# Storing layer 1's sums of x and no-op rows once, and a half-size block first among layer 0's experts

## The chip, the core and the metric

The kernel runs on one core of a Trainium2 chip. The metric is device time of one execution, in microseconds (us). Engines are named as in the profile: PE (TensorE matmuls) and PEld (its weight loads), DVE (VectorE), ACT (ScalarE), POOL (GpSimd) and SP (SyncE, which here only issues DMAs; its queue is SPq). SBUF is the on-chip memory, PSUM the accumulators that PE writes.

## What is computed

Two gated transformer layers over x (8 x 256 tokens of 256 numbers, 2048 tokens). The part that matters here, cut from the reference:

```python
x = x + tanh(g_xattn[0]) * L0_xattn(layernorm(x), ctx, ...)
x = x + tanh(g_ffn[0]) * L0_ffn(layernorm(x), ...)      # 8 experts, top 2, no capacity
x = x + tanh(g_xattn[1]) * L1_xattn(layernorm(x), ctx, ...)
x = x + tanh(g_ffn[1]) * L1_ffn(layernorm(x), ...)      # 7 experts and a no-op one, top 2

# L1_ffn: expert i takes its first cap = 256 tokens
h = relu(einsum('ceh,ehi->cei', inputs, experts_inter))
out = einsum('cei,eih->ceh', h, experts_out) * in_w[..., None]
combined = zeros_like(x_flat).at[used_idx].add(out.reshape(-1, hidden))
combined = combined + x_flat * (noop_w * noop_mask)[:, None]
```

So the result of layer 1 is x, plus the scaled no-op rows (normalised x times the weight of the eighth expert), plus the experts' rows, added token by token.

## The kernel before

Each layer is an attention phase and then a route and experts phase. A token tile is 128 tokens, on the 128 partitions; there are 16 (`TT`). `shared["x"]` (x_sb in the profile) holds x and `shared["xr"]` its normalised rows, 16 x 256 numbers on each partition.

**Attention** ends, for each of 8 batches, with `store_router_rows`: SP stores the normalised rows (L269, to the table normalised_weighted) and then x itself (L271), in layer 0 to x1, in layer 1 to out. The phase's last waits on SP are for those stores (L291, L292).

**Routing** (`route_phase`) is a chain of small DVE steps that finds for every slot of every block the token that belongs there (`token_of`). In layer 1 ACT also scales xr by the weight of the no-op expert (L1258), 16 instructions. The scratch tiles of this phase lie in x_sb, which in the kernel before is free by then because x is in memory, and in a small tile "more".

**Experts** (`expert_phase`) runs over blocks. A block has one expert's weights (w1 and w2, 1 MB each) and 256 rows (two gathers of 128) or, in layer 0 alone, 128 rows (one gather): a small block. Layer 0 has 16 full blocks and 7 small ones, and `SMALL_AT` says at which places of the 23 the small ones stand. Layer 1 has 7 full blocks. In a block b

- POOL gathers the rows of xw into `xe` (`load_x`, L1556), two buffers, and after the block scatters the weighted outputs with an adding DMA (`add_to_tokens`, L1581);
- PE turns the rows (`turn`, L1786), does the first product into ps_h (L89 to L91, each product split in three) and the second into ps_y. Its order is: first product of b, within it the turn of b + 1, then the second product of b - 1;
- ACT and DVE split weights, inputs and hidden rows in a high and a low part: ACT makes the high parts (L1616, L1624, L1656) and the activation (L1632, L1635), DVE the rest (L1688, L1699, L1711, L1713, L1757);
- the weights come by gathers of POOL in layer 0 (L1161) and by DMAs of SP in layer 1 (L1538 for w1, L1541 for w2), each as soon as the buffer two blocks back has been split.

No scheduler sets an order: each engine's program is written out, as above, and engines meet in semaphores. In layer 1 POOL's program begins with `load_x(0)`, `load_x(1)`, `load_x(2)`, then four DMAs of 512 KB that add the scaled no-op rows to out in memory (L1596), then for each b `load_x(b + 3)` and `add_to_tokens(b)`. The first `add_to_tokens` waits until the four DMAs have landed (`out_added`).

The functions that the change touches, and what calls them, follow with the line numbers of the profile.

Of the kernel before, what the change touches and what calls it, by code (L numbers as in the profile page):

```python
# [13 lines left out]
P = 128  # L14
B, S, D = 8, 256, 256
N = B * S
# [12 lines left out]


FULLS = 16
SMALL_AT = (3, 7, 10, 13, 16, 19, 22)
L0_BLOCKS = FULLS + len(SMALL_AT)
CT = 4
HALVES = 2 * FULLS + len(SMALL_AT)
# [65 lines left out]
def attention_phase(nc, layer, shared, dram):  # L101
# [4 lines left out]
    with ExitStack() as ctx:  # L106
# [105 lines left out]
        def _(sp):  # L212
# [48 lines left out]
                    sp.dma_start(dram["xw"][unused_rows, D:D + E], shared["zeros"][:, 0:E]).then_inc(xr_stored, 16)  # L261
            xr_dst = dram["xw"][0:N, 0:D].rearrange("(t p) d -> p t d", p=P)

            x_dst = dram["out" if layer else "x1"][0:N, :].rearrange("(t p) d -> p t d", p=P)

            def store_router_rows(b):
                tiles = slice(b * QT, b * QT + QT)
                wait_routed(sp, b)
                sp.dma_start(xr_dst[:, tiles, :], xr[:, tiles, :]).then_inc(xr_stored, 16)  # L269
                sp.wait_ge(x_done, b + 1)  # L270
                sp.dma_start(x_dst[:, tiles, :], x[:, tiles, :]).then_inc(x_stored, 16)  # L271

            load_context(4)
            maxima_to_slots(0)
# [14 lines left out]
            store_router_rows(B - 2)  # L289
            store_router_rows(B - 1)  # L290
            sp.wait_ge(xr_stored, 16 * (B + (0 if layer else 2 * QT)))  # L291
            sp.wait_ge(x_stored, 16 * B)  # L292

        @block.gpsimd
        def _(pool):
# [841 lines left out]
def expert_buffers(nc, ctx, layer):  # L1137

    sem = semaphores(nc, ctx)

    def sb(name, shape, dt=F32):
        return ctx.enter_context(nc.sbuf_tensor(f"{name}_w{layer}", shape, dt))

    def pair(name, shape):
        return [sb(f"{name}{i}", shape) for i in range(2)]

    buffers = {"w1_raw": pair("w1_raw", [P, KC * F + (0 if layer else FC)]),
               "w2_raw": pair("w2_raw", [P, FC * D + (0 if layer else D)]),
               "w1_ld": [sem(f"w1_ld{i}_w{layer}") for i in range(2)], "w2_ld": [sem(f"w2_ld{i}_w{layer}") for i in range(2)]}
    buffers["comb"] = sb("comb", [P, TT, E])  # L1150
    if layer:
        buffers["out_added"], buffers["noop_scaled"] = sem("out_added_w1"), sem("noop_scaled_w1")
    else:
        buffers["block_is"] = sb("block_is", [P, L0_BLOCKS, E])
    return buffers
# [10 lines left out]
def route_phase(nc, ctx, layer, shared, dram, buffers, tiles):  # L1166
# [2 lines left out]
    tg = shared["tanh_g"][:, 2 + layer:3 + layer]  # L1169


    spare = [shared["x"][:, :, :].rearrange("p a b -> p (a b)"), tiles["more"][:, :]]
    room = [TT * D, MORE]
    taken = [0, 0]

    def sb(name, shape, dt=F32, home=0):
        n = math.prod(shape[1:])
        words = n if dt in (F32, I32) else n // 2
        at = taken[home]
        taken[home] += words  # L1180
        assert taken[home] <= room[home], name
        ap = spare[home][:, at:at + words]
        if dt != F32:
            ap = ap.bitcast(dt)
        if len(shape) == 3:
            ap = ap.rearrange("p (a b) -> p a b", b=shape[2])
        if len(shape) == 4:
            ap = ap.rearrange("p (a b c) -> p a b c", b=shape[2], c=shape[3])
        return ap
# [21 lines left out]
    low, smaller = sb("low", [P, TT, E]), sb("smaller", [P, L0_BLOCKS])  # L1211
    before, first = sb("before", [P, 2, E, E]), sb("first", [P, E])
    base, place, valid = sb("base", [P, E]), sb("place", [P, TT, E]), sb("valid", [P, TT, E])
    past, blk_row, blk_expert = sb("past", [P, L0_BLOCKS, 2 * E], home=1), sb("blk_row", [P, L0_BLOCKS]), sb("blk_expert", [P, L0_BLOCKS])
    weight, slot = ([sb(f"{n}{i}", [P, TT], dt) for i in range(2)] for n, dt in (("weight", F32), ("slot", I32)))
    quotient, remainder = sb("quotient", [P, 2, TT], I32), sb("remainder", [P, 2, TT], I32)
    half_of, lane_of = sb("half_of", [P, 2, TT], F16), sb("lane_of", [P, 2, TT], F16)

    is_half = [sb(f"is_half{i}", [P, HALVES, TT], F16, i) for i in range(2)]
    token_at = [sb(f"token_at{i}", [P, HALVES, TT], F16) for i in range(2)]  # L1220
    is_lane = [sb(f"is_lane{i}", [P, P, TT], F16, i) for i in range(2)]
    unused = sb("unused", [P, HALVES])


# [248 lines left out]
def expert_phase(nc, ctx, layer, shared, dram, buffers):  # L1473
# [15 lines left out]
    def sem(name):  # L1489
        return new_sem(f"{name}_e{layer}")  # L1490
# [12 lines left out]
    if layer == 0:  # L1503
# [10 lines left out]
    w1_hi, w1_ready, w2_hi, w2_ready, xe_ps, xe_hi, xe_ready, h_ps, hid_ready, h_hi, h_ready, y_ps, y_ready = (  # L1514
        sem(n) for n in ("w1_hi", "w1_ready", "w2_hi", "w2_ready", "xe_ps", "xe_hi", "xe_ready", "h_ps",
                         "hid_ready", "h_hi", "h_ready", "y_ps", "y_ready"))
    last_ps, last_ready = sem("last_ps"), sem("last_ready")
    NP = FC // 2

    def loaded(b):  # L1520
# [3 lines left out]
        return 16 * sum(order[c][2] for c in range(b % 2, b + 1, 2))  # L1524

    listed, comb_stored = sem("listed"), sem("comb_stored")
    tiles = {"more": sb("more", [P, MORE]), "ps_h": ps_h, "ps_y": ps_y, "listed": listed, "comb_stored": comb_stored}

    def sync_part(sp):
        if layer:  # L1530

            for b in range(2):
                sp.wait_ge(xe_ld[b], passed(b))

            def load_weights(b):
                if b + 2 < blocks:
                    sp.wait_ge(w1_ready, b + 1)
                    sp.dma_start(w1_raw[b % 2][:, :], dram["w1"][(b + 2) * P:(b + 3) * P, :]).then_inc(w1_ld[b % 2], 16)  # L1538
                if b + 1 < blocks:
                    wait(sp, w2_ready, b)  # L1540
                    sp.dma_start(w2_raw[(b + 1) % 2][:, :],  # L1541
                                 dram["w2"][(b + 1) * P:(b + 2) * P, :]).then_inc(w2_ld[(b + 1) % 2], 16)

            for b in range(blocks):
                load_weights(b)
        for b in (blocks - 2, blocks - 1):
            sp.wait_ge(y_out[b % 2], passed(b))

    def pool_part(pool):
# [20 lines left out]
        def add_to_tokens(b):  # L1570
            if b < blocks - 1:
                pool.wait_ge(y_ready, b + 1)
            if b:
                pool.wait_ge(y_out[(b - 1) % 2], passed(b - 1))
            elif layer:
                pool.wait_ge(buffers["out_added"], 16 * (TT // CT))
            for q in range(order[b][2]):
                t = order[b][1] + q
                if b == blocks - 1:
                    pool.wait_ge(last_ready, q + 1)  # L1580
                pool.indirect_dma_start(  # L1581
                    out=dram["out" if layer else "x1"], out_offset=bass.IndirectOffsetOnAxis(ap=shared["token_of"][:, t:t + 1], axis=0),
                    in_=y[b % 2][:, q, :], in_offset=None, compute_op=ALU.add).then_inc(y_out[b % 2], 16)
# [3 lines left out]
        load_x(0)  # L1587
        load_x(1)
        if layer:
            load_x(2)  # L1590

            out_dst = dram["out"][0:N, :].rearrange("(t p) d -> p t d", p=P)
            for c in range(TT // CT):
                tiles = slice(c * CT, c * CT + CT)
                pool.wait_ge(buffers["noop_scaled"], c * CT + CT)
                pool.dma_start(out_dst[:, tiles, :], shared["xr"][:, tiles, :],  # L1596
                               accum_op=ALU.add).then_inc(buffers["out_added"], 16)
            for b in range(blocks):
# [353 lines left out]
```

## Time and profile before

| | us |
|---|---|
| median of 3 runs | 845.72 |
| lowest and highest | 845.16 and 845.79 |
| the profiled execution | 845.71 |
| its span in the trace | 844.0 |
| PE busy in it | 752.9 (89%) |
| DVE busy | 603.9 (72%) |
| ACT busy | 478.4 (57%) |
| POOL busy | 382.4 (45%) |

The span is 1.7 us less than that execution's own time; this rest lies outside the trace. The trace shows layer 0's attention up to 210 us, its routing up to 233, its experts up to 492, layer 1's attention up to 710, its routing up to 730 and its experts to the end. Times in the trace are from the span's start. The busy shares are averages over these stages. What a change is worth is read from the stage, from which wait ends last there.

### The profile page before, as it was taken

The numbers are of one execution on the slowest core, as the hardware profiler recorded it, in microseconds if no ns is written. First come the engines' busy times: TensorE is split into PE (matmuls) and PEld (weight loads), VectorE is DVE, ScalarE is ACT, GpSimd is POOL, SyncE is SP. The second block draws the span as 40 slices with busy tenths as digits, with TensorE's granted clock in tenths as the row PEclk, the third lists the DMA queues.
The fourth block names the chain that finished last, engine by engine and source line by source line (L and its number), as shares of the span: only waits on it lengthen the run. The fifth ranks groups of instructions, "written<-read, shape, count | busy, mean of one in ns | idle before, by whom it ended". The sixth has DMA issues, their size and how long they took to land. (4 is left out here: it accounts for less than half of the span.)

```text
span 844.0 us, 17413 instructions
## 1 busy us (share of the span) xinstructions
PE 752.9 (89%) x6872; PEld 636.0 (75%) x6872; DVE 603.9 (72%) x1212; ACT 478.4 (57%) x722; POOL 382.4 (45%) x379
## 2 busy tenths in 40 slices
PE   6999999999469999999999948999999998295995
PEld 5666667667369999999999946666677667295995
DVE  4777777753769998998998916777777734774882
ACT  3376666753056777777676603676667661553640
POOL 6465444112145766666666326645551130252532
PEclk9999999999779999999999979999999999587998
DMA  7001000010377888888888336001000013398642
GB/s 231 15 21 40 27 27 23 9 50 32 98 276 218 243 259 251 256 251 253 254 254 253 74 58 192 14 15 40 27 28 27 28 43 117 97 304 220 165 86 28
DMA packets 47697, 103.45 MB, mean 123 GB/s; under 512 B 9952, under 2 KB 38240, under 8 KB 39936
## 3 DMA queue, kind: packets, MB, share of 16 engines
q0 software_dynamic: 18912, 67.56, 28.0%
q1 hardware_dynamic: 28704, 34.78, 12.3%
q8 instruction: 55, 0.90, 0.4%
q14 instruction: 26, 0.21, 0.1%
HBM read 84.22 MB, written 17.83 MB: 121 GB/s over the span
## 5 line engine op out<-in xcount | busy, mean ns | idle before, releaser
L598 DVE TENSOR_REDUCE mx_a<-ps_max_a 128x2 f32<-128x512 f32 x256 | 164.2, 685 | 35.5 <-PE ps_max_a L844 35.2
L89 PE MATMUL ps_h_e<-xe_t_e,w_e 128*128 128x256 f32 (+1 forms) x480 | 137.9, 287 | 6.0 <-DVE xe_t_e L1757 6.0
L450 ACT ACTIVATE prob_a<-ps_st_a 128x2048 f32<-128x2048 f32 x64 | 120.1, 1876 | 29.1 <-PE ps_st_a L863 28.7
L90 PE MATMUL ps_h_e<-xe_t_e,w_e 128*128 128x256 f32 (+1 forms) x480 | 134.9, 281 | 0.0
L91 PE MATMUL ps_h_e<-xe_t_e,w_e 128*128 128x256 f32 (+1 forms) x480 | 134.9, 281 | 0.0
L89 PE MATMUL ps_y_e<-w_e,h_e 128*128 128x256 f32 x424 | 118.5, 279 | 0.0
L90 PE MATMUL ps_y_e<-w_e,h_e 128*128 128x256 f32 x424 | 118.0, 278 | 0.0
L91 PE MATMUL ps_y_e<-w_e,h_e 128*128 128x256 f32 x424 | 117.9, 278 | 0.0
L89 PEld LDWEIGHTS ps_h_e<-xe_t_e,w_e 128*128 128x128 f32 x480 | 93.0, 194 | 8.2 <-DVE xe_t_e L1757 8.2
L91 PEld LDWEIGHTS ps_h_e<-xe_t_e,w_e 128*128 128x128 f32 x480 | 92.7, 193 | 0.0
L90 PEld LDWEIGHTS ps_h_e<-xe_t_e,w_e 128*128 128x128 f32 x480 | 92.7, 193 | 0.0
L844 PE MATMUL ps_max_a<-k_r_a,q_r_a 32*128 32x512 f32 x256 | 82.8, 513 | 4.0 <-DVE mx_a L598 1.1
L318 POOL TENSOR_SCALAR r_var_eps_a<-r_mean_var_a 128x2 f32<-128x2 f32 x16 | 3.6, 228 | 180.0 <-DVE r_mean_var_a L625 180.0
L1161 POOL DMA_INDIRECT w_raw_w<-L_w,block_row x46 | 48.5, 1055 | 80.6 <-DVE b_e L1704 55.4
L1581 POOL DMA_INDIRECT x<-y_e,token_of x39 | 68.6, 1760 | 30.7 <-ACT y_e L1647 17.4
L1556 POOL DMA_INDIRECT xe_e<-normalised_weighted,token_of x53 | 61.7, 1163 | 45.4 <-DVE token_of L1467 28.0
L89 PEld LDWEIGHTS ps_y_e<-w_e,h_e 128*128 128x128 f32 x424 | 79.9, 188 | 0.0
L91 PEld LDWEIGHTS ps_y_e<-w_e,h_e 128*128 128x128 f32 x424 | 79.9, 188 | 0.0
L90 PEld LDWEIGHTS ps_y_e<-w_e,h_e 128*128 128x128 f32 x424 | 79.8, 188 | 0.0
L1713 DVE TENSOR_TENSOR h_e<-hid_e,h_e 128x512 fp32r<-128x512 f32 (+1 forms) x120 | 76.1, 634 | 4.1
L863 PE MATMUL ps_st_a<-q_s_a,k_s_a 32*128 32x256 f32 x1024 | 78.0, 395 | 0.3
L1635 ACT ACTIVATE hid_e<-ps_h_e,b_e 128x256 f32<-128x256 f32 (+1 forms) x184 | 71.0, 445 | 8.1 <-PE ps_h_e L91 7.6
(236 smaller groups left out, 1756.0 us busy)
## 6 DMA issues: line engine op xcount, KB each, us to landing
w_raw_w<-L_w SPq DMA_DIRECT2D x14, 1024.0 KB
ctx_raw_a<-ctx_t SPq DMA_DIRECT2D x16, 256.0 KB, 4.2
normalised_weighted<-xr SPq DMA_DIRECT2D x16, 256.0 KB, 2.2
x_sb<-x SPq DMA_DIRECT2D x8, 256.0 KB
x_sb<-x SPq DMA_DIRECT2D x2, 1024.0 KB, 8.6
x<-x_sb SPq DMA_DIRECT2D x8, 256.0 KB, 2.5
out<-x_sb SPq DMA_DIRECT2D x8, 256.0 KB, 2.5
out<-xr POOLq DMA_DIRECT2D x4, 512.0 KB, 21.9
```

Of the source, the lines that this page charges most:

```text
L89: pe.matmul(out, lhs[0], rhs[0], start=start, stop=False)
L90: pe.matmul(out, lhs[1], rhs[0], start=False, stop=False)
L91: return pe.matmul(out, lhs[0], rhs[1], start=False, stop=stop)
L450: act.activation(prob[n % 2][:, :, :, :], ps_st[:, :, :, :], ACT.Exp, scale=HD ** -0.5).then_inc(prob_ready, 1)
L598: dve.tensor_reduce(mx[:, q, h:h + HG + 1:HG], ps_max[j][:, :, :], AX.X, ALU.max).then_inc(max_done, 1)
L844: pe.matmul(ps_max[j][:, :, :], q_r[b % 2][r:r + 32, c, q * P:(q + 1) * P], k_r[b % 2][r:r + 32, c, :, :], start=True, stop=True).then_inc ...
L863: ins = pe.matmul(ps_st[:, g, kt, :], k_s[b % 3][c % 2][rows, c // 2, kt * P:(kt + 1) * P], q_s[b % 3][c % 2][rows, c // 2, :], start=True ...
L1161: pool.indirect_dma_start(out=buffers[which + "_raw"][b % 2][:, :], out_offset=None, in_=dram[which], in_offset=bass.IndirectOffsetOnAxis( ...
L1556: pool.indirect_dma_start(out=xe[b % 2][:, q, :], out_offset=None, in_=dram["xw"], in_offset=bass.IndirectOffsetOnAxis(ap=shared["token_of ...
L1581: pool.indirect_dma_start(out=dram["out" if layer else "x1"], out_offset=bass.IndirectOffsetOnAxis(ap=shared["token_of"][:, t:t + 1], axis=0),
L1635: ins = act.activation(hid[jp % 2][:, j, 0:w], ps_h[jp % RB][:, j, 0:w], ACT.Gelu, bias=b1[b % 2][:, 2 * jp + j:2 * jp + j + 1])
L1713: dve.tensor_tensor(h[b % 2][1][:, js, 0:w], hid[jp % 2][:, :, 0:w], h[b % 2][0][:, js, 0:w].bitcast(F32), ALU.subtract).then_inc(h_ready, 1)
```

## The change

It has four parts.

1. `SMALL_AT` goes from (3, 7, 10, 13, 16, 19, 22) to (0, 4, 8, 12, 15, 18, 22).
2. Layer 1's attention no longer stores x to out.
3. In layer 1's experts, the no-op rows are added to x in SBUF by POOL, four additions of 128x1024 (`add_rows`), and the sums are stored to out by SP, four plain DMAs of 512 KB. The first `add_to_tokens` waits for these (`out_stored`).
4. So that x_sb stays intact, the scratch tiles of routing lie elsewhere (in "more", in hid, y and xe of the experts, and in w2_raw's second buffer), in both layers.

```diff
-SMALL_AT = (3, 7, 10, 13, 16, 19, 22)
+SMALL_AT = (0, 4, 8, 12, 15, 18, 22)
...
                 sp.dma_start(xr_dst[:, tiles, :], xr[:, tiles, :]).then_inc(xr_stored, 16)
-                sp.wait_ge(x_done, b + 1)
-                sp.dma_start(x_dst[:, tiles, :], x[:, tiles, :]).then_inc(x_stored, 16)
+                if layer == 0:
+                    sp.wait_ge(x_done, b + 1)
+                    sp.dma_start(x_dst[:, tiles, :], x[:, tiles, :]).then_inc(x_stored, 16)
...
-            sp.wait_ge(x_stored, 16 * B)
+            if layer == 0:
+                sp.wait_ge(x_stored, 16 * B)
...
-    spare = [shared["x"][:, :, :].rearrange("p a b -> p (a b)"), tiles["more"][:, :]]
-    room = [TT * D, MORE]
-    taken = [0, 0]
+    spare = [tiles["more"][:, :]] + [tile[:, :, :].rearrange("p a b -> p (a b)") for tile in tiles["later"]]
+    spare.append(buffers["w2_raw"][1][:, 0:FC * D])
+    room = [MORE] + [math.prod(tile.shape[1:]) for tile in tiles["later"]] + [FC * D]
+    taken = [0] * len(spare)
...
+            out_dst = dram["out"][0:N, :].rearrange("(t p) d -> p t d", p=P)
             for b in range(blocks):
                 load_weights(b)
+                if b == 0:
+                    for c in range(TT // CT):
+                        sp.wait_ge(out_summed, c + 1)
+                        tiles = slice(c * CT, c * CT + CT)
+                        sp.dma_start(out_dst[:, tiles, :], shared["x"][:, tiles, :]).then_inc(buffers["out_stored"], 16)
...
             elif layer:
-                pool.wait_ge(buffers["out_added"], 16 * (TT // CT))
+                pool.wait_ge(buffers["out_stored"], 16 * (TT // CT))
...
         if layer:
-            load_x(2)
-
-            out_dst = dram["out"][0:N, :].rearrange("(t p) d -> p t d", p=P)
-            for c in range(TT // CT):
+
+            def add_rows(c):
                 tiles = slice(c * CT, c * CT + CT)
                 pool.wait_ge(buffers["noop_scaled"], c * CT + CT)
-                pool.dma_start(out_dst[:, tiles, :], shared["xr"][:, tiles, :],
-                               accum_op=ALU.add).then_inc(buffers["out_added"], 16)
+                pool.tensor_tensor(shared["x"][:, tiles, :], shared["x"][:, tiles, :], shared["xr"][:, tiles, :],
+                                   ALU.add).then_inc(out_summed, 1)
+
+            add_rows(0)
+            add_rows(1)
+            load_x(2)
+            add_rows(2)
+            add_rows(3)
             for b in range(blocks):
                 load_x(b + 3)
                 add_to_tokens(b)
```

How this moves instructions, at three places. In the names, xe0_e1 is the first buffer of gathered rows in layer 1's experts, y0_e1 a block's weighted output.

POOL at the start of layer 1's experts, before:

```order
L1845 UNCONDITIONAL_BRANCH
L1556 DMA xe0_e1<-normalised_weighted,token_of 128x264 x2
L1556 DMA xe1_e1<-normalised_weighted,token_of 128x264 x2
L1556 DMA xe0_e1<-normalised_weighted,token_of 128x264 x2
L1596 DMA out<-xr 128x4x256 x4
L1556 DMA xe1_e1<-normalised_weighted,token_of 128x264 x2
L1581 DMA out<-y0_e1,token_of 2304x256 x2
```

And in the changed kernel:

```order
L1858 UNCONDITIONAL_BRANCH
L1565 DMA xe0_e1<-normalised_weighted,token_of 128x264 x2
L1565 DMA xe1_e1<-normalised_weighted,token_of 128x264 x2
L1603 TENSOR_TENSOR x_sb<-x_sb,xr 128x1024 x2
L1565 DMA xe0_e1<-normalised_weighted,token_of 128x264 x2
L1603 TENSOR_TENSOR x_sb<-x_sb,xr 128x1024 x2
L1565 DMA xe1_e1<-normalised_weighted,token_of 128x264 x2
L1590 DMA out<-y0_e1,token_of 2304x256 x2
```

Four adding DMAs between the third and the fourth pair of gathers are gone; two POOL additions stand ahead of the third pair and two ahead of the fourth.

SP from the start of layer 1's routing on, before (w_raw is a block's raw weights):

```order
L1240 DMA normalised_weighted<-comb_w1 128x16x8
L1538 DMA w1_raw0_w1<-L1_w1 128x2048
L1541 DMA w2_raw1_w1<-L1_w2 128x2048
L1538 DMA w1_raw1_w1<-L1_w1 128x2048
L1541 DMA w2_raw0_w1<-L1_w2 128x2048
```

And in the changed kernel:

```order
L1243 DMA normalised_weighted<-comb_w1 128x16x8
L1541 DMA w1_raw0_w1<-L1_w1 128x2048
L1544 DMA w2_raw1_w1<-L1_w2 128x2048
L1554 DMA out<-x_sb 128x4x256 x4
L1541 DMA w1_raw1_w1<-L1_w1 128x2048
L1544 DMA w2_raw0_w1<-L1_w2 128x2048
```

The four stores, each with a wait for one of POOL's additions, stand ahead of the weights w1 of block 3 and all later ones.

POOL at the start of layer 0's experts, before:

```order
L1161 DMA w1_raw1_w0<-L0_w1,block_row 128x2056
L1556 DMA xe0_e0<-normalised_weighted,token_of 128x264 x2
L1556 DMA xe1_e0<-normalised_weighted,token_of 128x264 x2
L1161 DMA w1_raw0_w0<-L0_w1,block_row 128x2056
L1161 DMA w2_raw1_w0<-L0_w2,block_row 128x2304
```

And in the changed kernel:

```order
L1163 DMA w1_raw1_w0<-L0_w1,block_row 128x2056
L1565 DMA xe0_e0<-normalised_weighted,token_of 128x264
L1565 DMA xe1_e0<-normalised_weighted,token_of 128x264 x2
L1163 DMA w1_raw0_w0<-L0_w1,block_row 128x2056
L1163 DMA w2_raw1_w0<-L0_w2,block_row 128x2304
```

Block 0 has one gather instead of two, and everything behind it on POOL is issued one gather earlier.

## Rows read from the trace of the kernel before

**Rows 1.** The page's first line.

```profile
span 844.0 us, 17413 instructions
```

**Rows 2.** Waits from 725 us on: who waited for whom, us in total, times, longest.

```profile
POOL out L1581 <- DMA out<-xr: 22.7, 1, 22.7
PE ps_x_e L1786 <- DMA xe_e<-normalised_weighted,token_of: 16.8, 2, 10.2
```

**Rows 3.** The chain that ended last: start us, us, what.

```profile
748.25 24.28 DMA xe_e<-normalised_weighted,token_of
```

**Rows 4.** Timeline of POOL, layer 1: start us, us, instruction, [idle before <-releaser].

```profile
735.45 0.94 POOL L1556 DMA_INDIRECT xe_e<-normalised_weighted,token_of  x1 [0.30 <-issue]
738.58 0.94 POOL L1556 DMA_INDIRECT xe_e<-normalised_weighted,token_of  x1 [2.18 <-DVE xe_t_e L1757]
...
740.77 5.37 POOL L1596 DMA_DIRECT2D out<-xr  x4
746.44 1.50 POOL L1556 DMA_INDIRECT xe_e<-normalised_weighted,token_of  x1 [0.30 <-issue]
748.25 1.81 POOL L1556 DMA_INDIRECT xe_e<-normalised_weighted,token_of  x1 [0.30 <-issue]
```

**Rows 5.** Tile xe_e, the two gathers that POOL issued from 738 to 741.

```profile
DMA to landing us min/median/max: 6.4/6.6/6.8
```

**Rows 6.** DMA issues of the page: count, KB each, median us to landing.

```profile
out<-xr POOLq DMA_DIRECT2D x4, 512.0 KB, 21.9
```

**Rows 7.** Stretches: length, busy us (count) by engine, PE clock, DMA share, GB/s.

```profile
core 0: us, PE busy (x) PEld busy (x) DVE busy (x) ACT busy (x) POOL busy (x), PEclk, DMA share, GB/s
750.66:786.32 35.66, 25.45 (x202) 25.25 (x201) 23.16 (x36) 13.99 (x20) 7.74 (x6) 0.86 0.81 222
786.32:797.87 11.55, 11.55 (x102) 11.55 (x101) 10.40 (x17) 6.45 (x10) 6.76 (x5) 1.00 0.79 224
762.36:772.57 10.21, 0.00 (x1) 0.00 (x0) 4.66 (x7) 0.79 (x2) 0.00 (x0) 0.72 0.91 284
309.49:341.58 32.09, 31.77 (x276) 31.57 (x275) 29.61 (x55) 22.96 (x45) 21.21 (x16) 1.00 0.83 247
```

**Rows 8.** Timeline of PE, in both layers' experts.

```profile
238.67 1.13 PE L1786 MATMUL ps_x_e<-ident,xe_e 128*128 128x128 f32 x4 [5.68 <-DMA xe_e<-normalised_weighted,token_of]
261.40 0.38 PE L89 MATMUL ps_h_e<-xe_t_e,w_e 128*128 128x256 f32 x1 [0.85 <-DVE xe_t_e L1757]
757.96 0.28 PE L89 MATMUL ps_h_e<-xe_t_e,w_e 128*128 128x256 f32 x1
772.57 1.13 PE L1786 MATMUL ps_x_e<-ident,xe_e 128*128 128x128 f32 x4 [10.21 <-DMA xe_e<-normalised_weighted,token_of]
```

**Rows 9.** Timeline of DVE, layer 1 first, then a small block of layer 0.

```profile
741.96 0.74 DVE L1711 CAST h_e<-hid_e 128x512 fp32r<-128x512 f32 x1 [3.65 <-ACT hid_e L1632]
742.73 0.69 DVE L1713 TENSOR_TENSOR h_e<-hid_e,h_e 128x512 fp32r<-128x512 f32 x1
744.68 0.43 DVE L1711 CAST h_e<-hid_e 128x512 fp32r<-128x512 f32 x1 [0.59 <-ACT hid_e L1632]
756.82 0.69 DVE L1757 TENSOR_TENSOR xe_t_e<-ps_x_e,xe_t_e 128x512 fp32r<-128x512 f32 x1
276.99 0.30 DVE L1711 CAST h_e<-hid_e 128x256 fp32r<-128x256 f32 x1 [0.34 <-ACT hid_e L1635]
277.32 0.42 DVE L1713 TENSOR_TENSOR h_e<-hid_e,h_e 128x256 fp32r<-128x256 f32 x1
```

**Rows 10.** Groups of POOL by form: busy us, mean ns, idle before.

```profile
L314 POOL TENSOR_TENSOR x_sb<-x_sb,tgbo_a 128x512 f32<-128x512 f32 x16 | 20.4, 1283 | 0.7
```

**Rows 11.** Timeline of SP's queue in layer 1's experts.

```profile
739.14 0.43 SPq L1538 DMA_DIRECT2D w_raw_w<-L_w  x1
749.20 0.33 SPq L1541 DMA_DIRECT2D w_raw_w<-L_w  x1
```

**Rows 12.** Waits of SP's queue, whole span.

```profile
SPq L292 <- DMA out<-x_sb: 2.0, 1, 2.0
```

**Rows 13.** Timeline of POOL at the start of layer 0's experts.

```profile
233.81 1.69 POOL L1556 DMA_INDIRECT xe_e<-normalised_weighted,token_of  x1 [4.53 <-DVE token_of L1467]
235.80 0.95 POOL L1556 DMA_INDIRECT xe_e<-normalised_weighted,token_of  x1 [0.30 <-issue]
```

More of the change, by code:

```diff
@@ L262, in _ @@
             xr_dst = dram["xw"][0:N, 0:D].rearrange("(t p) d -> p t d", p=P)
-            x_dst = dram["out" if layer else "x1"][0:N, :].rearrange("(t p) d -> p t d", p=P)
+            x_dst = dram["x1"][0:N, :].rearrange("(t p) d -> p t d", p=P)
             def store_router_rows(b):
@@ L1151, in expert_buffers @@
     if layer:
-        buffers["out_added"], buffers["noop_scaled"] = sem("out_added_w1"), sem("noop_scaled_w1")
+        buffers["out_stored"], buffers["noop_scaled"] = sem("out_stored_w1"), sem("noop_scaled_w1")
     else:
@@ L1169, in route_phase, with sb @@
     tg = shared["tanh_g"][:, 2 + layer:3 + layer]
-    spare = [shared["x"][:, :, :].rearrange("p a b -> p (a b)"), tiles["more"][:, :]]
-    room = [TT * D, MORE]
-    taken = [0, 0]
-    def sb(name, shape, dt=F32, home=0):
+    spare = [tiles["more"][:, :]] + [tile[:, :, :].rearrange("p a b -> p (a b)") for tile in tiles["later"]]
+    spare.append(buffers["w2_raw"][1][:, 0:FC * D])
+    room = [MORE] + [math.prod(tile.shape[1:]) for tile in tiles["later"]] + [FC * D]
+    taken = [0] * len(spare)
+    def sb(name, shape, dt=F32):
         n = math.prod(shape[1:])
         words = n if dt in (F32, I32) else n // 2
+        home = [i for i in range(len(spare)) if taken[i] + words <= room[i]][0]
         at = taken[home]
         taken[home] += words
-        assert taken[home] <= room[home], name
         ap = spare[home][:, at:at + words]
@@ L1213, in route_phase @@
     base, place, valid = sb("base", [P, E]), sb("place", [P, TT, E]), sb("valid", [P, TT, E])
-    past, blk_row, blk_expert = sb("past", [P, L0_BLOCKS, 2 * E], home=1), sb("blk_row", [P, L0_BLOCKS]), sb("blk_expert", [P, L0_BLOCKS])
+    past, blk_row, blk_expert = sb("past", [P, L0_BLOCKS, 2 * E]), sb("blk_row", [P, L0_BLOCKS]), sb("blk_expert", [P, L0_BLOCKS])
     weight, slot = ([sb(f"{n}{i}", [P, TT], dt) for i in range(2)] for n, dt in (("weight", F32), ("slot", I32)))
@@ L1217, in route_phase @@
     half_of, lane_of = sb("half_of", [P, 2, TT], F16), sb("lane_of", [P, 2, TT], F16)
-    is_half = [sb(f"is_half{i}", [P, HALVES, TT], F16, i) for i in range(2)]
+    is_half = [sb(f"is_half{i}", [P, HALVES, TT], F16) for i in range(2)]
     token_at = [sb(f"token_at{i}", [P, HALVES, TT], F16) for i in range(2)]
-    is_lane = [sb(f"is_lane{i}", [P, P, TT], F16, i) for i in range(2)]
+    is_lane = [sb(f"is_lane{i}", [P, P, TT], F16) for i in range(2)]
     unused = sb("unused", [P, HALVES])
@@ L1516, in expert_phase @@
                          "hid_ready", "h_hi", "h_ready", "y_ps", "y_ready"))
-    last_ps, last_ready = sem("last_ps"), sem("last_ready")
+    last_ps, last_ready, out_summed = sem("last_ps"), sem("last_ready"), sem("out_summed")
     NP = FC // 2
@@ L1526, in expert_phase @@
     listed, comb_stored = sem("listed"), sem("comb_stored")
-    tiles = {"more": sb("more", [P, MORE]), "ps_h": ps_h, "ps_y": ps_y, "listed": listed, "comb_stored": comb_stored}
+    tiles = {"more": sb("more", [P, MORE]), "later": hid + y + xe, "ps_h": ps_h, "ps_y": ps_y, "listed": listed, "comb_stored": comb_stored}
     def sync_part(sp):
```

## The prediction, made before the changed kernel ran

> **What bounds the kernel now.** I read four views, from the end backwards. The chain that ended last has one link that is neither PE nor a short step: a gather of rows for the experts of layer 1, issued at 748.25, that is 24.28 us on its way [rows 3]. The waits of that stage say who paid: PE waited 10.2 us for such a gather, in one piece, and POOL 22.7 us for the adding DMAs of the no-op rows before it could scatter the first block [rows 2]. POOL's timeline shows the cause in its order: the gathers of block 3 (746.44 and 748.25) are issued right behind the four adding DMAs (740.77) [rows 4]. Those take a median of 21.9 us to land [rows 6], while the gathers issued two us ahead of them landed in 6.4 to 6.8 us, though a weight load of 1 MB, the last of three in a row, had been issued at 739.14 [rows 5, 11]. So the queue of adding DMAs is what the gathers sit behind, not the weights.
>
> What this costs is read from the stretches. From the turn of block 2 (750.66) to the turn of block 4 (786.32) are 35.66 us; one later block takes 11.55 us, with PE busy all of it and DVE 10.40 [rows 7]. Two blocks should be 23.1, so **12.6 us** are lost: 10.2 of idle PE, and 2.4 in the matmuls behind it, where the granted clock was down from 2.4 to 1.2 GHz (the mean over the idle stretch is already 0.72) [rows 7, 8]. Elsewhere in the expert stages PE is busy nearly throughout, so nothing but a PE gap is worth anything there. The reader should also see how little spare DVE has early on: block 2's first product starts at 757.96, and the DVE instruction that it needs last runs from 756.82 for 0.69, that is, until 757.5 [rows 8, 9]. The margin is 0.45 us.
>
> **Layer 1, what goes.** The four adding DMAs go from POOL's queue, 5.4 us of issuing with them [rows 4]. Without them the third pair of gathers runs as below, and the stall of 12.6 us goes if its data are there when PE reaches 762.4.
>
> **Layer 1, what comes.** Four additions of 128x1024 on POOL. The nearest row is an addition of 128x512 at 1.28 us [rows 10]; twice that is 2.56 each, 10.2 in all. Placed in POOL's order: the second pair of gathers ends at 736.4 [rows 4], so two additions run to 741.6. The third pair (block 2) is issued at 741.9 and 743.2 rather than 738.58; with 6.6 us to landing it is there by 749.8, ahead of the turn at 750.66, with 0.9 to spare. The other two additions run from 744.1 to about 749.7 with their waits, and the pair for block 3 is issued from 750.0 to 753.6 (at the 1.50 and 1.81 of rows 4). With up to 6.8 us to landing it is there by 758.7, ahead of 762.4. SP's stores wait for the additions, and the load of w1 for block 3 waits behind them: from 739.14 to about 750 [rows 11]. The w2 load behind it was issued at 749.20 anyhow and moves by 1 us. ACT first needs w1 of block 3 when it has begun block 2, around 759; two stores (1 MB) and this load at the 284 GB/s of rows 7 take 7 us, until 757. That is cover enough, but it is no large one: 1 us later per us that the additions slip beyond 2. All four stores land by then too, before the first scatter can start (760), so the wait of 22.7 us is worth nothing more by itself.
>
> **What the additions do to DVE** is the term that the trace does not show: no DVE instruction that reads two SBUF tiles runs there beside a POOL computation. The first two additions fall where DVE waits for PE (its instruction of 741.96 had idled 3.65 us) [rows 9]. The other two fall at 744.1, just as DVE begins the unbroken run of casts and subtractions that ends in the margin of 0.45. Lower bound: nothing, then the gain is all 12.6. Upper bound: the two engines exclude each other and DVE stands still for what of both additions falls in its run: 746.7 minus 744.7 for the first, 2.5 for the second, 4.5 us. The nearest row is a DVE cast beside POOL's DMA issues: 0.74 instead of 0.43, while POOL's own gather issues beside DVE's run took 1.50 and 1.81 instead of 0.94 [rows 4, 9]. Each delays the other, which looks like exclusion for as long as POOL touches SBUF; an addition touches it all the time. I take the upper bound, 4.5, less the margin 0.45: **a new PE gap of 4.1 us** ahead of block 2's first product (part of it may show ahead of block 0's second product, which waits for the same run). Layer 1's experts then gain 12.6 - 4.1 = **8.5 us**.
>
> The Trainium skill, page "SBUF — State Buffer", section "Who interferes with whom", says that a DVE instruction with two SBUF inputs and a GpSimd one that reads SBUF share a port pair, and that the one that starts second "fully blocks". By the 0.3 us of the row alone the gap would be nearly nothing; by the page it would be the 4.1 above. No row here shows a case of the page's own kind.
>
> **Layer 0, small block first.** Block 0 now needs one gather. The second was issued 2.0 us after the first, whose issue took 0.74 longer [rows 13], so the first should land some 1.25 us before 238.67, when PE started. Two transposes instead of four and half-width copies on ACT and DVE take off another 0.8 (the four took 1.13) [rows 8]. Then DVE bounds: block 2's first product waited 0.85 us for it at 261.40 [rows 8]. DVE's cast and subtraction take 0.30 + 0.42 in a small block instead of 0.43 + 0.69 [rows 9], 0.4 less, four times: 1.6. So 261.40 becomes about 257.7, 3.7 earlier. Not all of it is gain, since a small block's saving is spent here instead of at place 3: two full blocks and a small one took 32.09 us [rows 7], so a small one 32.09 - 23.1 = 9.0, 2.6 less than a full one. Net 3.7 - 2.6 = 1.1, and I take **1.2**. Bounds: -1.0, if the start does not come earlier, and 2.5, if PE and not DVE bounds again. How the other small blocks are spread costs nothing that the trace shows: PE is busy 31.77 of the 32.09, and the last block is small in both.
>
> **The rest.** SP's last wait of the attention, for the store of x, was 2.0 us [rows 12]. The engines' own work ended about when it did, so I count 0.2 (bounds 0 and 2.0). The eight stores of x in layer 1's attention lie beside PE work and are counted at nothing; so is the scratch's new place, since no instruction's shape changes. The sum is 8.5 + 1.2 + 0.2 = 9.9. Against the profiled execution, 844.0 of span and 1.7 around it [rows 1], which is the median within 0.01 us: 845.7 - 9.9 = **835.8**.
>
> **The rivals.**
>
> *No exclusion.* DVE runs its subtractions beside POOL's additions with little loss; block 2's gap is under 0.5. Gain 12.5 + 1.4 = 13.9, **831.8**. For it: the subtraction behind the slow cast took its usual 0.69 while POOL was still issuing [rows 4, 9]. Against it: the rows with 0.74, 1.50 and 1.81.
>
> *Exclusion and more.* The small copy of DVE that belongs to block 0's inputs stands beside the first addition, which would hold block 0's first product by up to 1.4 us; and a gap of 4 us lets the clock fall as after the 10.2 us one, another 2.4. Gain 8.5 - 3.8 + 1.4 = 6.1, **839.6**. The 0.85 us gap in layer 0 left no mark; a gap of this size is not in the trace.
>
> *Starved additions, slower than before.* If DVE's unbroken run keeps POOL out, rather than taking turns, the last two additions wait for its end, which is at 767.0 (4.66 busy from 762.36) [rows 7], and block 3's gathers stand behind them: 767.0 + 5.1 for the additions + 2.5 for the two issues + 3.6 to landing = 778.2, against 772.57 now. That is 5.7 us more stall, less 1.4: **850.0**. It decides as soon as POOL gets no turn for more than some 8 us. Against it: POOL's gather issues in that very run took 0.6 to 0.9 us longer, not more.
>
> *The gathers stay slow.* If it is the sum of traffic that held block 3's gather for 24.28 us, it still does: issued at 751.8, landing at 776.1, 3.5 later than now, less 1.4: **847.8**. Against it: the 6.4 to 6.8 us of the pair before, at a traffic that was as heavy [rows 5].
>
> **How the numbers follow.** The forecast (one gap of about 4 us in place of one of 10 with its slow clock) has 0.48, with its own range 833.5 to 838; no exclusion 0.27; exclusion and more 0.15; starved additions 0.06; slow gathers 0.03; and 0.01 for losses that cancel. The range reaches over the first three, with layer 0's bounds at either end: 830.5 to 840.5. About 0.2%, 1.7 us, is what a measurement of this kernel can tell from no change. Faster by more than that: 0.90; within: 0.02; slower: 0.08.
>
> **What would show it.** In the changed kernel's PE timeline the idle of 10.21 us ahead of block 3's turn should be gone, and the granted clock should not fall there. POOL's third and fourth additions should lie beside stretched DVE instructions (a subtraction of 0.69 as one of 2 to 3 us) and a PE gap ahead of block 2's first product should be released by DVE. If they are not stretched, the no-exclusion rival holds. If the additions themselves take 5 us or more, it is the starved one. In layer 0 PE's first turn should start near 237.4 and block 2's first product near 257.7. I am wrong outright if block 3's turn still waits for its gather, or if PE waits for weights of block 3 that SP sent late.

## The result and the profile after

| | us | ratio to before |
|---|---|---|
| before, 5 runs | 845.72 (845.16 to 846.47) | |
| changed kernel, 5 runs | 841.34 (840.39 to 844.63) | 0.9954, 95% interval 0.9941 to 0.9967 |
| its profiled execution | 844.63, span 842.8 | |

The change makes the kernel 4.4 us faster. The forecast was 9.9 us, and its range ended 0.8 us below the measured median, so the prediction was too optimistic. Of the missing 5.5 us, layer 0 took most and layer 1 the rest.

**Layer 1.** PE's timeline of the changed kernel: start us, us, instruction, what it had idled and for whom. Behind the first turn these are the only rows with a wait up to block 3's turn at 773.37, which has none.

```profile
741.37 1.13 PE L1799 MATMUL ps_x_e<-ident,xe_e 128*128 128x128 f32 x4 [6.68 <-DMA xe_e<-normalised_weighted,token_of]
747.34 0.58 PE L89 MATMUL ps_h_e<-xe_t_e,w_e 128*128 128x256 f32 x1 [4.83 <-DVE xe_t_e L1770]
...
756.30 0.39 PE L89 MATMUL ps_h_e<-xe_t_e,w_e 128*128 128x256 f32 x1 [1.45 <-DVE xe_t_e L1770]
...
769.02 0.39 PE L89 MATMUL ps_h_e<-xe_t_e,w_e 128*128 128x256 f32 x1 [0.66 <-DVE xe_t_e L1770]
```

The 10.21 us ahead of block 3's turn [rows 8] are gone. In their place are three waits for DVE, ahead of the first products of blocks 0, 1 and 2. In the kernel before only block 0's first product waited for DVE, block 1's did not, nor block 2's [rows 8]:

```profile
738.36 0.58 PE L89 MATMUL ps_h_e<-xe_t_e,w_e 128*128 128x256 f32 x1 [1.48 <-DVE xe_t_e L1757]
```

The timelines of POOL and of DVE in the changed kernel show what held DVE:

```profile
742.02 4.64 POOL L1603 TENSOR_TENSOR x_sb<-x_sb,xr 128x1024 f32<-128x1024 f32 x2
747.56 0.96 POOL L1565 DMA_INDIRECT xe_e<-normalised_weighted,token_of  x1 [0.90 <-DVE xe_t_e L1770]
748.83 0.95 POOL L1565 DMA_INDIRECT xe_e<-normalised_weighted,token_of  x1 [0.30 <-issue]
749.80 4.75 POOL L1603 TENSOR_TENSOR x_sb<-x_sb,xr 128x1024 f32<-128x1024 f32 x2
```

```profile
743.17 3.52 DVE L1764 COPY slot_weight_e<-xe_e 128x2 f32<-128x2 f32 x1 [3.39 <-ACT xe_t_e L1669]
746.61 0.68 DVE L1770 TENSOR_TENSOR xe_t_e<-ps_x_e,xe_t_e 128x512 fp32r<-128x512 f32 x1
750.94 3.90 DVE L1724 CAST h_e<-hid_e 128x512 fp32r<-128x512 f32 x1 [3.65 <-ACT hid_e L1645]
```

Each pair of additions holds one DVE instruction until the second of them has ended: 742.02 + 4.64 = 746.66, where the copy ends at 746.69; 749.80 + 4.75 = 754.55, where the cast ends at 754.84. Without a POOL addition beside them they take 0.17 and 0.43 us (rows of the experiment with the additions on DVE, below).

The stretch from block 0's first product to the last matmul, before and after, shows the sum: length, busy us (count) by engine, PE clock, DMA share, GB/s.

```profile
738.36:833.84 95.48, 85.27 (x696) 84.86 (x696) 66.95 (x105) 40.96 (x58) 39.75 (x26) 0.92 0.66 174
```

```profile
747.34:832.68 85.34, 83.22 (x696) 82.62 (x696) 69.53 (x105) 41.11 (x58) 38.78 (x24) 0.98 0.64 185
```

It is 10.1 us shorter, that is the stall of 12.6 less two gaps of 2.1 and a rest of 0.4. But it begins 3.4 us later after its turn (a wait of 4.83 instead of 1.48), so layer 1's experts gained 6.8 us.

**Layer 0.** The last matmul of its experts before, then in the changed kernel:

```profile
490.81 0.28 PE L91 MATMUL ps_y_e<-w_e,h_e 128*128 128x256 f32 x1
```

```profile
493.52 0.28 PE L91 MATMUL ps_y_e<-w_e,h_e 128*128 128x256 f32 x1
```

The stage ends 2.7 us later, where 1.2 earlier was forecast. PE's timeline shows why.

```profile
238.22 0.70 PE L1799 MATMUL ps_x_e<-ident,xe_e 128*128 128x128 f32 x2 [5.18 <-DMA xe_e<-normalised_weighted,token_of]
240.12 0.47 PE L89 MATMUL ps_h_e<-xe_t_e,w_e 128*128 128x128 f32 x1 [1.20 <-DVE xe_t_e L1770]
...
251.21 0.52 PE L89 MATMUL ps_h_e<-xe_t_e,w_e 128*128 128x256 f32 x1
...
255.32 0.28 PE L90 MATMUL ps_h_e<-xe_t_e,w_e 128*128 128x256 f32 x1
```

And the granted clock in two stretches of the kernel before, then in two of the changed kernel (columns as above):

```profile
239.00:244.68 5.68, 3.98 (x19) 3.58 (x18) 3.35 (x6) 2.71 (x4) 4.46 (x5) 0.50 0.72 237
244.68:250.00 5.32, 5.32 (x48) 5.32 (x47) 3.90 (x8) 3.95 (x9) 0.98 (x2) 1.00 0.97 387
```

```profile
238.22:255.25 17.03, 15.83 (x73) 15.44 (x74) 11.06 (x22) 9.36 (x18) 7.89 (x7) 0.50 0.69 237
255.25:266.13 10.88, 10.88 (x95) 10.88 (x95) 10.50 (x20) 8.15 (x15) 4.63 (x4) 1.00 0.64 228
```

PE starts its first product 1.4 us earlier than before (240.12 against 241.50), but the granted clock stays at 1.2 GHz until 255.25. In the kernel before it rose to 2.4 GHz at 244.68, some 3.2 us into the first product of a full block. In the changed kernel all 48 matmuls of the small block's first product run at 1.2 GHz, with PE busy throughout, and the rise comes 4.0 us into block 1. A small block's first product has 48 matmuls, as many as a full one's, and at the low clock one starts every 0.21 us in either. So it saves PE nothing there; its saving lies in its second product, which has 24 matmuls instead of 48 and starts at 259.16, when the clock is up. 10.6 us at half the rate is 5.3 us of lost matmul time.

**The profiled execution** is 3.3 us above the median. Most of this lies in neither part. At the start of layer 1's attention, two DVE instructions took 3.42 us (before, 1.03) beside work of POOL that is the same in both kernels:

```profile
510.65 0.60 POOL L337 CAST ctx_t_hi_a<-ctx_raw_a 128x512 fp32r<-128x512 f32 x1
511.33 1.27 POOL L339 TENSOR_TENSOR ctx_t_lo_a<-ctx_raw_a,ctx_t_hi_a 128x512 fp32r<-128x512 f32 x1
512.54 1.45 POOL L354 MEMSET v_a<- 128x512 f32 x3
```

```profile
510.72 3.42 DVE L581 TENSOR_SCALAR xn_a<-x_sb,mean_var_a,rstd_a 128x256 f32<-128x256 f32 x2 [1.27 <-POOL rstd_a L303]
```

Here POOL's cast began 0.07 us ahead of DVE's first instruction, and DVE's two ended at 514.14, 0.15 us behind POOL's last memset. So it looks like the same hold. In the profile of before and in the nine of the experiments DVE began first, by 0.10 to 0.78 us, and the same two instructions take 0.73 to 1.16 us. I read it as chance which of them begins first; that was not tested.

### The profile page after: what moved, and what is told of

The parts are those of the page before. It is cut to its first block and busy times, and to the rows that moved or that the text cites. A ratio compares the mean times of both kernels' runs of the same rounds, so it can differ in the third digit from the quotient of the medians.

```text
span 842.8 us, 17408 instructions
## 1 busy us (share of the span) xinstructions
PE 758.0 (90%) x6872; PEld 641.5 (76%) x6872; DVE 612.7 (73%) x1212; ACT 477.8 (57%) x722; POOL 384.7 (46%) x379
## 3 DMA queue, kind: packets, MB, share of 16 engines
q1 hardware_dynamic: 28640, 34.78, 12.6%
## 5 line engine op out<-in xcount | busy, mean ns | idle before, releaser
L89 PE MATMUL ps_h_e<-xe_t_e,w_e 128*128 128x256 f32 (+1 forms) x480 | 139.8, 291 | 9.8 <-DVE xe_t_e L1770 9.8
L91 PE MATMUL ps_h_e<-xe_t_e,w_e 128*128 128x256 f32 (+1 forms) x480 | 137.0, 285 | 0.0
L90 PE MATMUL ps_h_e<-xe_t_e,w_e 128*128 128x256 f32 (+1 forms) x480 | 136.9, 285 | 0.0
L89 PEld LDWEIGHTS ps_h_e<-xe_t_e,w_e 128*128 128x128 f32 x480 | 95.1, 198 | 12.0 <-DVE xe_t_e L1770 12.0
L90 PEld LDWEIGHTS ps_h_e<-xe_t_e,w_e 128*128 128x128 f32 x480 | 94.4, 197 | 0.0
L91 PEld LDWEIGHTS ps_h_e<-xe_t_e,w_e 128*128 128x128 f32 x480 | 94.4, 197 | 0.0
```

What stands on the lines that cost most here:

```text
L89: pe.matmul(out, lhs[0], rhs[0], start=start, stop=False)
L90: pe.matmul(out, lhs[1], rhs[0], start=False, stop=False)
L91: return pe.matmul(out, lhs[0], rhs[1], start=False, stop=stop)
```

## The experiments

### One part at a time: the sums alone

The changed kernel with the small blocks at their old places.

```diff
-SMALL_AT = (0, 4, 8, 12, 15, 18, 22)
+SMALL_AT = (3, 7, 10, 13, 16, 19, 22)
```

> The changed kernel with SMALL_AT as before: only layer 1's part (sums of x and no-op rows on POOL, stored once by SP). Theory: the change's two parts have opposite signs. Layer 1's part gains what its trace shows from the list of tokens to the end, 114.5 us before and 107.8 after, so 6.8, and layer 0's part loses some 2 to 3. Then this kernel takes 838.9 us, and POOL's two pairs of additions still hold DVE's small copy (3.5 us) and its first cast (3.9 us). Rival: layer 0's part costs nothing and layer 1's gains only the 4.4 us of the whole: 841.3 us.

Measured: 838.46 us (837.55 to 839.93), before 845.47 in the same session, ratio 0.9911 (0.9891 to 0.9931). The sums alone gain 7.0 us. Copy and cast are held as in the changed kernel, for 3.53 and 3.88 us.

### The small block first, alone

The kernel before with the new `SMALL_AT`.

> The kernel before with the new SMALL_AT alone. Theory: the small block at place 0 leaves the granted clock at 1.2 GHz until a full block's matmuls run (it rose at 255.3 us in the changed kernel, at 244.7 in the one before), which costs 2.7 us by the end of layer 0's experts: 848.4 us. Rival, my prediction's own step: the start comes earlier and the time falls by 1.2, to 844.5.

Measured: 848.59 us (848.02 to 851.15), ratio 1.003 (1.0016 to 1.0045). This part makes the kernel 3.1 us slower: -7.0 + 3.1 = -3.9, where both together give -4.4. The parts add up. Its trace repeats layer 0 of the changed kernel; until the rise and behind it:

```profile
238.10:255.00 16.90, 15.70 (x72) 15.31 (x73) 10.95 (x22) 9.22 (x18) 7.76 (x7) 0.50 0.68 237
255.00:262.00 7.00, 7.00 (x62) 7.00 (x61) 6.86 (x13) 6.40 (x11) 1.90 (x2) 1.00 0.78 299
```

### Is it the spreading, or the first place?

The kernel before with the same spreading, but the small block second.

```diff
-SMALL_AT = (3, 7, 10, 13, 16, 19, 22)
+SMALL_AT = (1, 4, 8, 12, 15, 18, 22)
```

> The kernel before with SMALL_AT = (1, 4, 8, 12, 15, 18, 22): the small block at place 1, the others spread as in the change. Theory of the clock: block 0 is a full one again and raises the clock at about 245 us, so the loss of e2_small_only is gone: 845.7 within 1 us. Rival: the loss comes from how the others are spread, or from DVE's tight run at the start; then it is there here too, at 848 us.

Measured: 845.89 us (845.27 to 847.82), ratio 1.0001 (0.999 to 1.0013). The loss is gone, and the clock rises where it did in the kernel before:

```profile
238.70:244.53 5.83, 4.13 (x19) 3.73 (x19) 3.35 (x6) 2.77 (x4) 3.99 (x4) 0.50 0.84 289
244.53:255.00 10.47, 10.47 (x93) 10.47 (x93) 9.59 (x18) 9.40 (x20) 3.41 (x4) 1.00 0.65 224
```

Spreading costs nothing, as the prediction said. What costs is a small block's first product at the time at which the clock has yet to rise.

### The clock raised beforehand

The changed kernel, with 22 transposes on PE behind the last matmuls of layer 0's routing, while it waits for block 0's gather, and 6 while it waits for DVE. Their results are used by nobody.

```diff
+        if layer == 0:
+            fill(22)
...
         turn(0)
+        if layer == 0:
+            keep_busy(pe, ps_y[0][:, 0, 0:P], ident, 6)
         first_product(0)
```

> The changed kernel with idle work for PE at the start of layer 0's experts: 22 transposes of 128x128 (results unused) between the routing's last matmuls and the first turn, and 6 behind it. Theory of the clock: the transposes raise the granted clock before block 0, the small block's products then run at 2.4 GHz, and what layer 0's part lost (2.7) comes back, with some 1 us of the gain I had predicted: 837 to 838 us against 841.3. Rival: the clock is not what the small block costs; then the time stays at 841.3 or rises by what the transposes delay the turn.

Measured: 837.82 us (835.63 to 841.47), before 845.21, ratio 0.9915 (0.989 to 0.9939): 3.5 us less than the changed kernel. Granted clock and PE's timeline, then the end of layer 0's experts:

```profile
238.35:255.25 16.90, 15.66 (x136) 15.23 (x134) 15.56 (x30) 15.33 (x28) 10.87 (x9) 1.00 0.83 304
```

```profile
239.72 0.33 PE L89 MATMUL ps_h_e<-xe_t_e,w_e 128*128 128x128 f32 x1 [0.55 <-DVE xe_t_e L1772]
256.32 0.38 PE L89 MATMUL ps_h_e<-xe_t_e,w_e 128*128 128x256 f32 x1 [1.76 <-DVE xe_t_e L1772]
...
488.07 0.28 PE L91 MATMUL ps_y_e<-w_e,h_e 128*128 128x256 f32 x1
```

In the same stretch PE now does 136 matmuls, 6 of them transposes of the filling, where the changed kernel did 73. A matmul of the small block now starts every 0.11 us, again as one of a full block does. Block 2's first product is bounded by DVE, as the prediction had it, and starts at 256.32. The stage ends 5.5 us earlier than in the changed kernel (488.07 against 493.52), close to the 5.3 us of lost matmul time: the late clock is what layer 0 paid for.

That the stage ends 2.7 us earlier than in the kernel before is not what the small block is worth, since the kernel before has no transposes in its place. By medians this kernel gains 0.6 us on the sums alone with the old places (837.82 against 838.46), and the ranges overlap. Its six executions also fall in two groups: 835.6 to 836.4 us at a mean granted clock of 0.958 to 0.960, and 839.3 to 841.5 at 0.949 to 0.955. The profile is one of the first group. So the same kernel does not keep its clock in every execution alike.

### The additions on the other engine

The sums alone, with the four additions made by DVE, two on each side of block 0's inputs (the lines with a minus are POOL's, those with a plus DVE's).

```diff
-            add_rows(0)
-            add_rows(1)
             load_x(2)
-            add_rows(2)
-            add_rows(3)
...
+                if layer:
+                    add_rows(0)
+                    add_rows(1)
                 inputs_low(b)
+                if layer:
+                    add_rows(2)
+                    add_rows(3)
```

> As e1_sums_only, but the four additions of 128x1024 run on DVE, two ahead of block 0's inputs and two behind them, where DVE waits for PE. Theory: what layer 1's part still loses is POOL holding DVE. On DVE an addition takes 1.1 to 1.2 us (as its 128x1024 subtractions do), 4.8 in all, inside waits of 3.3 and 3.7 us. The copy is back at 0.2 us and the cast at 0.4; the time is 845.7 - 12.5 = 833 us, 5 to 6 less than e1_sums_only. Rival: the stall in layer 1 is from the order of SP's stores and weights, then this kernel is no faster than e1_sums_only.

Measured: 834.06 us (833.2 to 835.82), ratio 0.986 (0.9838 to 0.9883), 4.4 us less than with the additions on POOL. DVE's timeline, and the only wait of PE between its first turn and 770 us:

```profile
734.02 2.35 DVE L1752 TENSOR_TENSOR x_sb<-x_sb,xr 128x1024 f32<-128x1024 f32 x2
737.44 0.17 DVE L1759 COPY slot_weight_e<-xe_e 128x2 f32<-128x2 f32 x1 [1.06 <-ACT xe_t_e L1658]
...
738.11 2.35 DVE L1752 TENSOR_TENSOR x_sb<-x_sb,xr 128x1024 f32<-128x1024 f32 x2
741.85 0.43 DVE L1713 CAST h_e<-hid_e 128x512 fp32r<-128x512 f32 x1 [1.39 <-ACT hid_e L1634]
```

```profile
738.25 0.58 PE L89 MATMUL ps_h_e<-xe_t_e,w_e 128*128 128x256 f32 x1 [1.48 <-DVE xe_t_e L1765]
```

An addition takes DVE 1.2 us, half of POOL's 2.32, and all four fit where DVE waited for ACT. The holds and the gaps are gone: they did come from POOL's additions. The gain over the sums alone, 4.4 us, is less than the 5 to 6 expected.

### The small copy on ACT

The sums alone, with the 128x2 copy made by ACT in layer 1.

```diff
+            if layer:
+                act.activation(slot_weight[:, b, :], xe[b % 2][:, :, D + b], ACT.Copy)
...
-            if layer:
-                dve.tensor_copy(slot_weight[:, b, :], xe[b % 2][:, :, D + b])
-            else:
+            if not layer:
```

> e1_sums_only (additions on POOL), but the small copy of the slots' weights (128x2) is done by ACT instead of DVE. Theory: POOL's first two additions then hold nobody, block 0's first product starts 3.4 us earlier, while the last two still hold DVE's cast, now a little less or in the midst of its run: 835.5 us against 838.5, leaving 1.5 to e3_dve_adds. If exclusion were only a matter of long instructions and not of this copy, ACT's copy would change nothing: 838.5.

Measured: 836.92 us (835.9 to 839.75), before 845.21, ratio 0.99 (0.9882 to 0.9919). The gain is 1.5 us over the copy on DVE, not 3, and the ranges overlap. DVE's timeline; the additions run from 737.33 to 742.00 and from 744.41 to 749.16:

```profile
738.60 0.69 DVE L1770 TENSOR_TENSOR xe_t_e<-ps_x_e,xe_t_e 128x512 fp32r<-128x512 f32 x1 [3.51 <-ACT xe_t_e L1671]
742.94 0.43 DVE L1726 CAST h_e<-hid_e 128x512 fp32r<-128x512 f32 x1 [3.65 <-ACT hid_e L1645]
...
746.02 3.43 DVE L1726 CAST h_e<-hid_e 128x512 fp32r<-128x512 f32 x1 [1.25 <-ACT hid_e L1645]
```

The subtraction that has one operand in PSUM runs through the middle of the additions in its usual 0.69 us. So block 0's first product is as early as in the kernel before (1.50 behind its turn). The hold hits the next cast, with two gaps of 0.70 and 1.22 us on PE behind it. That accounts for part of the shortfall, and differences between executions may be the rest.

### What a waiting instruction waits for

The sums alone, with one addition ahead of block 2's gathers and three behind.

```diff
             add_rows(0)
-            add_rows(1)
             load_x(2)
+            add_rows(1)
             add_rows(2)
             add_rows(3)
```

> The experiment with the sums alone, and POOL's four additions in another order: one ahead of block 2's pair of gathers and three behind it, where it was two and two. The question is what a waiting DVE instruction waits for. If it waits for all additions that stand in a row on POOL: the small copy ahead of block 0's inputs, 3.53 us in the sums-alone kernel, is held by one addition only and takes 1.0 to 1.5 us, so block 0's first product starts some 2.3 us earlier after its turn (gap 2.5 instead of 4.84); the cast behind the first activation, 3.88 us there, is held by three additions, from about 742.8 to 748.5, and takes 5.5 to 6 us. The run of DVE behind it then starts as late as before, and the total stays about the same: 838.5, between 837.5 and 839.5. If instead a waiting DVE instruction gets in as soon as one addition ends, the copy takes 1.0 to 1.5 too, but the cast 2 us at most, DVE's run begins some 3.5 us earlier, and the total is about 836.0. If the hold does not come from the additions at all, the copy takes 3.5 again and the total stays at 838.5.

Measured: 839.54 us (838.36 to 839.81), before 845.77, ratio 0.9914 (0.9896 to 0.9933). The first theory's durations hold to 0.2 us, and the total lies just above the upper end of what it gave, 839.5. POOL and DVE:

```profile
737.18 2.35 POOL L1603 TENSOR_TENSOR x_sb<-x_sb,xr 128x1024 f32<-128x1024 f32 x1
...
742.65 7.05 POOL L1603 TENSOR_TENSOR x_sb<-x_sb,xr 128x1024 f32<-128x1024 f32 x3
```

```profile
738.31 1.25 DVE L1764 COPY slot_weight_e<-xe_e 128x2 f32<-128x2 f32 x1 [3.37 <-ACT xe_t_e L1669]
...
743.81 6.19 DVE L1724 CAST h_e<-hid_e 128x512 fp32r<-128x512 f32 x1 [3.65 <-ACT hid_e L1645]
```

One addition holds the copy for its own rest. Three in a row hold the cast for 6.19 us, until 0.3 after their end: a waiting DVE instruction does not get in between them. PE's wait for block 0's inputs falls from 4.84 to 2.56 us, and a wait of 2.44 us ahead of block 1's first product takes back what that gained.

### Both remedies together

The additions on DVE and the transposes in both layers, with the old places of the small blocks and then with the new ones.

> e3_dve_adds (old SMALL_AT) with the same idle work for PE in both layers. Theory: block 0's turn and the first quarter of its product run at 2.4 instead of 1.2 GHz in both layers, 1 to 2 us a layer before DVE bounds: 831 us against 834.1. Rival: DVE's run sets the start of block 2's product anyhow, and nothing is gained: 834.

Measured: 832.19 us (829.78 to 834.06), before 845.21, ratio 0.9829 (0.9811 to 0.9848). That is 1.9 us less than with the additions on DVE alone (834.06), and the ranges overlap. In its profile the transposes raised the clock, but it did not stay up. In layer 0 it was at 1.00 up to 241.15; behind the gap of 1.04 us ahead of block 0's first product it fell to 0.52 (241.15 to 244.20) and was up again from 244.70. In layer 1 its mean was 0.72 over the turn (735.25 to 737.40) and 0.50 from 737.48 to 741.00.

```profile
238.00:244.00 6.00, 4.25 (x23) 4.01 (x24) 3.35 (x6) 2.49 (x3) 4.48 (x6) 0.77 0.60 197
```

The last matmul of layer 0's experts starts at 489.80, where in the five profiles with the old places and no transposes (the kernel before among them) it starts between 490.08 and 491.30.

> e6_dve_fill with the new SMALL_AT. With the clock up at the start, the small block first has only the terms of my prediction left: a start 1 to 2 us earlier and DVE's shorter casts, less the small block's saving: 1.2 less than e6_dve_fill, 830. Rival: the small block's matmuls let the clock fall, or do not hold it; then it is 1 to 3 us more than e6_dve_fill.

Measured: **830.49 us** (828.99 to 833.87), ratio 0.9821 (0.9799 to 0.9843), the fastest kernel of this study, 15 us below the kernel before. The small block first now gains 1.7, but the ranges overlap. In its profile layer 0's last matmul starts at 489.86, no earlier than with the old places: behind a gap of 1.80 us the clock fell, and 36 matmuls took 5.82 us, where the same 36 took 4.21 in the changed kernel with transposes.

```profile
256.46:262.28 5.82, 5.82 (x36) 5.82 (x37) 5.58 (x9) 3.10 (x7) 3.66 (x3) 0.71 0.86 306
```

```profile
256.32:260.53 4.21, 4.21 (x36) 4.21 (x37) 4.01 (x7) 1.50 (x4) 2.35 (x2) 1.00 0.77 264
```

There the gap ahead was 1.76 us, and the clock stayed. What decides between them stays open; the length of the gap alone does not, since the clock fell behind 1.04 us in the kernel above. The clock fell somewhere in layer 0 in both profiles of this section, so what the small block first is worth with the clock up throughout has no fair comparison here, and stays open too.

## Why the prediction was too low

- **The stall of layer 1, 12.6 us: right.** The wait of 10.21 us and the low clock behind it are gone. POOL issues block 3's gathers at 756.51 and 757.79. Layer 1's first turn is 5.6 us later than before (741.37 against 735.75), so on the forecast's time scale that is 750.9 and 752.2, where 750.0 was the forecast for the first. No turn waits for them. So the adding DMAs were what delayed the gathers. Whether their queue was, as the prediction said, or their own traffic was not separated: the change moved them to another queue and made them plain stores at once. The rival of the slow gathers and that of the starved additions fell: an addition took 2.3 us, never 5.
- **The cost of the additions, 4.1 us: right in kind, too small, and in another place.** DVE does stand still, as the upper bound said. The step that failed is "The first two additions fall where DVE waits for PE". Between them stands the small copy, and it was held until both were done: 3.4 us ahead of block 0's first product. The rival "exclusion and more" had named this copy, but gave it 1.4 us, as if the first addition alone held it. The other two additions were to hold DVE for 4.5 us and leave a gap of 4.1 ahead of block 2. They held the first cast for 3.5, and the gaps came to 1.45 and 0.66 us. The subtractions, which were to be stretched, never met an addition. In sum -6.8 instead of -8.5 (by medians, with the attention's part, -7.0 instead of -8.7). The clock did not fall in these gaps. The second half of that rival, a clock that falls in a gap of 4 us, was not put to the test: the only gap of that length, 4.83 us, came while the clock was still low.
- **Layer 0, 1.2 us: wrong in sign.** Its start was earlier, but by less than forecast: PE's first turn by 0.45 us (238.22, where 237.4 was forecast and 238.67 was before), a third of the 1.25; the first product by 1.4 of 2.05. What failed is the step from there to 257.7 for block 2's first product: it came at 261.88. That step halved and shortened instructions of DVE and kept PE's matmuls at the times of before without saying so; rows 7 give the clock of later stretches alone, and when it rises at the start of the stage was not asked. It rose 10.6 us later. In the prediction's own sum block 2's first product came 0.5 us later instead of 3.7 earlier, and with the 2.6 of the small block's saving, spent here, that makes 3.1 later; the stage ended 2.7 later instead of 1.2 earlier. The bound of -1.0 allowed only for a start that is not earlier. With transposes that raise the clock beforehand, DVE is the bound again, and the stage ends 5.5 us earlier than without them.
- **The rest, 0.2 us:** it can't be told apart from the differences between executions.
- **The sum.** 3.1 us lost in layer 0 against 1.2 gained is 4.3 of the error, 1.7 in layer 1 the rest; together 6.0, and 5.5 are missing. Neither the forecast's own case nor any rival had a loss in layer 0, and the lower bound was that of the start alone. So the range ended too early.

The term that the prediction called unseen, a DVE instruction with two SBUF inputs beside a POOL computation, does not occur in the experts of the kernel before, but it does in the attention. These rows are from the start of layer 1's:

```profile
508.52 0.68 DVE L647 TENSOR_TENSOR wq_lo_a<-wq_raw_a,wq_hi_a 128x512 fp32r<-128x512 f32 x1
509.31 1.57 DVE L647 TENSOR_TENSOR wk_lo_a<-wk_raw_a,wk_hi_a 128x512 fp32r<-128x512 f32 x1
```

```profile
508.53 1.80 POOL L337 TENSOR_TENSOR ctx_t_lo_a<-ctx_raw_a,ctx_t_hi_a 128x512 fp32r<-128x512 f32 x1
510.28 1.44 POOL L352 MEMSET v_a<- 128x512 f32 x3
```

POOL's subtraction began 0.01 us behind DVE's first and took 1.80 us, where the same subtraction of layer 0, which DVE's did not precede (start 11.64), took 1.27. DVE's second began while POOL's ran and took 1.57 instead of 0.68, until 0.55 behind POOL's end, with the memset behind it no hindrance. So exclusion could be read before the change ran, and the rival "no exclusion", with its chance of 0.27, had a plain row against it.

Of the rules of the Trainium skill, page "SBUF — State Buffer", section "Who interferes with whom", the traces agree with four. A DVE copy or cast from SBUF to SBUF can be blocked, not slowed, by a GpSimd instruction that began first (3.52 and 3.90 us). A `tensor_tensor` of DVE with one SBUF input is not (0.69 us beside an addition, its other input in PSUM). One with two SBUF inputs contends with a GpSimd instruction that reads SBUF (1.57 us). And which one blocks the other goes by the order of issue (1.80 us of POOL, then 1.57 of DVE). The subtractions of the experts, on which the prediction laid the cost, met no addition.

## What to carry to other kernels

Before work goes to POOL, list every DVE instruction with all its operands in SBUF that can become ready while it runs, the smallest too, and price each at the end of the whole unbroken row of POOL instructions; a copy of 0.17 us that PE waits for cost 3.4 here. An engine that idles at the same time is a better home for it, even if it is the busier one on average. Where a stage begins after idle time of PE, look up when the granted clock rises, and what PE runs until then; an edit that makes the first pieces smaller can push the rise back by more than it saves.

## What the runs showed of the hardware

- A DVE copy of 128x2 (0.17 us by itself) is held by a POOL addition as a cast of 128x512 is. Two additions in a row held it 3.52 us, one 1.25; three held a cast 6.19 us. POOL's additions themselves kept their 2.32 to 2.38 us in every case.
- DVE and POOL instructions that both read two SBUF tiles exclude each other, whichever began second (0.68 became 1.57 us on DVE, 1.27 became 1.80 on POOL); a memset of POOL did not hold DVE's.
- A matmul of the first products starts every 0.21 us at 1.2 GHz and every 0.11 at 2.4 GHz, whether its output is 128x128 or 128x256.
- With PE busy without a break in a small block's first product, the granted clock stayed at 1.2 GHz for 11 us (240.12 to 251.15). With full blocks it rose after 3.2 and 4.0 us, and it was up at 238.35 behind the 22 transposes of 128x128. Behind a gap of 1.76 us the clock was kept, behind one of 1.80 us it fell, in two kernels whose layer 0 is the same, and in a third it fell behind 1.04 us; the traces give no reason.
